# Cross attention of a decoder with its sums laid out by query tile: tokens on the partitions, no copy and turn of the sums, and their bias as a row added by GpSimd

## The reference

```
tn = _ln(t, norm_g, norm_b)
t = _mha(tn, tn, skv, sq, sow, sob, tgt_mask) + t     # self attention, 16 heads of 64
tn = _ln(t, norm_g, norm_b)
t = _mha(src, tn, ckv, cq, cow, cob, src_mask) + t    # cross attention, 77 keys
tn = _ln(t, pg, pb)
t = t + (jax.nn.relu(tn @ w1 + b1) @ w2 + b2)         # 128 -> 512 -> 128
```

## Time and profile before

| | |
|---|---|
| median of 3 runs | 1062.11 us (1061.4 to 1063.75) |
| the profiled execution, its own time | 1062.09 us |
| its span in the profile | 1060.0 us |
| TensorE busy | 1025.4 us (97%) |
| ScalarE busy | 811.6 us (77%) |
| VectorE busy | 717.0 us (68%) |
| GpSimd busy | 393.8 us (37%) |

### The profile page before, as it was taken

How to read it: one execution, slowest core, us unless ns; L and a number is a source line. 1 busy time by engine, 2 the same in 40 slices (tenths; PEclk the granted TensorE clock), 3 DMA queues, 4 the chain that set the end, 5 groups by cost and what they waited for, 6 DMA issues and landing times.

```text
span 1060.0 us, 20691 instructions
## 1 busy us (share of the span) xinstructions
PE 1025.4 (97%) x5236; PEld 615.5 (58%) x5236; DVE 717.0 (68%) x4485; ACT 811.6 (77%) x3540; POOL 393.8 (37%) x407
## 2 busy tenths in 40 slices
PE   8899999999999999999999999999999999999996
PEld 6655556565456665545655555656655566555565
DVE  4766786556788566778665578655678755677845
ACT  4787997576998576899666799766799867689852
POOL 4233443233443233443333344323344323344322
PEclk9999999999999999999999999999999999999999
DMA  8322000003000002200003200001300000000000
GB/s 235 88 61 68 1 21 2 1 20 109 20 21 1 2 1 80 68 2 21 1 2 80 68 1 21 1 1 33 103 14 21 2 1 1 21 1 1 2 1 24
DMA packets 31818, 32.39 MB, mean 31 GB/s; under 512 B 3998, under 2 KB 27726, under 8 KB 30926
## 3 DMA queue, kind: packets, MB, share of 16 engines
q1 hardware_dynamic: 29390, 28.80, 9.4%
q10 hardware_dynamic: 2304, 2.20, 0.7%
HBM read 30.47 MB, written 0.52 MB: 29 GB/s over the span
## 4 chain that ended last, share of the span: by engine, by line
PE 86%; DVE 8%; issue 3%; ACT 1%; DVEq 1%; POOL 1%; POOLq 0%
PE S L1090 23%; PE T L1102 12%; PE sum L1132 10%; PE W L901 8%; PE sum L1116 7%; PE W L956 4%; PE W L925 4%; PE W L843 3%; PE W L880 3%; PE W L863 2%; PE W L858 2%; PE W L920 2%; DVE XN L1468 2%; DVE Pb L1620 2%; PE W L834 2%
## 5 line engine op out<-in xcount | busy, mean ns | idle before, releaser
L1382 ACT ACTIVATE Pb<-Pb,mn 128x128 f32<-128x128 f32 (+1 forms) x1536 | 560.5, 370 | 42.4 <-DVE mn L1620 42.1
L708 POOL TENSOR_TENSOR Pb<-Pb,rsum 128x512 f32<-128x512 f32 (+2 forms) x336 | 325.4, 971 | 582.3 <-DVE rsum L1628 582.3
L1382 ACT ACTIVATION_READ_ACCUMULATOR Pb<-Pb,mn 128x1 f32 x1536 | 293.0, 191 | 0.0
L1620 DVE CUSTOM_DVE_ANT_0 Pb<-S,late_bias 128x128 f32<-128x128 f32 x768 | 175.6, 285 | 130.4 <-PE S L1090 130.1
L1102 PEld LDWEIGHTS T<-ident,Pb 128*128 128x128 f32 (+2 forms) x1296 | 163.9, 146 | 155.1 <-issue 119.7
L1090 PE MATMUL S<-GV,XT 128*128 128x512 f32 x384 | 199.6, 607 | 1.6 <-DVE mn L1620 0.8
L1102 PE MATMUL T<-ident,Pb 128*128 128x128 f32 (+2 forms) x1296 | 197.4, 273 | 1.2 <-POOL Pb L708 1.2
L1638 DVE COPY PT<-T 128x512 f32<-128x512 f32 (+1 forms) x240 | 156.3, 651 | 57.1 <-PE T L1102 55.7
L1620 DVE CUSTOM_DVE_ANT_0 Pb<-S,cross_bias 128x77 f32<-128x77 f32 x768 | 132.4, 232 | 70.4 <-PE S L1090 68.0
L1132 PE MATMUL sum<-PT,Vc 128*128 128x512 f32 (+2 forms) x264 | 134.4, 599 | 0.0
L1090 PE MATMUL S<-Gc,XT 128*128 128x462 f32 (+1 forms) x288 | 126.7, 521 | 0.6 <-DVE mn L1620 0.5
(11 more groups left out here) (213 smaller groups left out, 1071.1 us busy)
## 6 DMA issues: line engine op xcount, KB each, us to landing
sakv<-in_L_xattn_sa_kv SPq DMA_DIRECT2D x6, 1024.0 KB, 5.0
caq<-in_L_xattn_ca_q SPq DMA_DIRECT2D x6, 512.0 KB, 8.0
saq<-in_L_xattn_sa_q SPq DMA_DIRECT2D x6, 512.0 KB, 6.2
cakv<-in_L_xattn_ca_kv SPq DMA_DIRECT2D x12, 256.0 KB, 7.8
saow<-in_L_xattn_sa_ow SPq DMA_DIRECT2D x6, 512.0 KB, 4.0
w<-in_L_xattn_ff_w SPq DMA_DIRECT2D x12, 256.0 KB, 3.0
caow<-in_L_xattn_ca_ow SPq DMA_DIRECT2D x30, 96.0 KB, 2.5
GV<-in_mask_BxSxS_ik ACTq DMA_DIRECT2D x1, 1536.0 KB, 9.3
```

Source lines behind the costliest of these rows:

```text
L708: nc.gpsimd.tensor_tensor(rows, rows, r, ALU.mult).then_inc(sem(f"{unit.name}_weights"), 1)
L1382: last = nc.scalar.activation(Pb[:, s, t * w:(t + 1) * w], Pb[:, s, t * w:(t + 1) * w], ACT.Exp, bias=mn[:, s, t:t + 1], scale=-1.0, accum ...
L1620: last = nc.vector.tensor_tensor_reduce(out=Pb[:, s, cols], in0=S_ps[n % 2][:, cols], in1=row_bias, scale=1.0, scalar=3.4e38, op0=ALU.add, ...
```

## The change

Cross attention goes by query tile. `place_of` gives each chunk its group and tile: in the cross phases the three groups of one tile follow on each other, then the next tile's. `attend_tokens(n)` runs after each turned chunk: the turned weights of one tile are the stationary operand, the values `Vc` move (128 columns), and the sums have tokens on the partitions. For this, ScalarE's copy and the job `fin` of the cross phases are left out; VectorE adds `sum_ps` to `X` itself (`cross_residual`), and this add now frees the bank. The bias `ca_ob` is loaded as a row to all partitions (`cob`) and added to `X` by GpSimd after the norm in front of the cross attention. The counterpart is done in `ending`. Some places on the tick list are changed too. `vT` shares the memory of `o_pair` (used in the other path only).

```diff
-CV0_AT = (13, 15, 18, 20, 26, 30)
-CV_AT = (4, 6, 7, 22, 26, 29)
-SELF1_AT = (23, 25, 26, 30)
+CV0_AT = (10, 12, 15, 16, 24, 27)
+CV_AT = (4, 6, 7, 20, 26, 29)
+SELF1_AT = (23, 24, 26, 30)
-WEIGHTS0_AT = (5, 3, 7, 10, 13, 16)
-WEIGHTS_AT = (20, 25, 30, 32, 33, 33, 35, 35, 38, 38, 40, 40, 43, 42, 45, 45)
-AFTER_S0 = (3, 4, 5, 5, 8, 9)
+WEIGHTS0_AT = (5, 3, 7, 12, 16, 18)
+WEIGHTS_AT = (20, 23, 30, 32, 33, 33, 35, 35, 37, 37, 40, 40, 43, 42, 45, 45)
+AFTER_S0 = (3, 4, 5, 5, 6, 7)
-LAST_AT = (1, 3, 5, 7)
+LAST_AT = (1, 3, 5, 9)
-FEED1 = ((9, 9, 9, 9), 10, (18, 18, 20, 21))
+FEED1 = ((9, 9, 9, 9), 12, (18, 18, 20, 21))
...
+            if self.groups[first].cross:
+                qt, group = divmod(n - first * TB, len(XHEADS))
+            self.place_of.append((self.groups[first + group], qt))
...
-            for blk in range(group.blocks):
+            for blk in range(TB):
+                if group.cross:
+                    self.attend[max(self.tick_of[g * TB + blk] + 1 + spread[group.phase % 4], self.start[group.j, group.phase % 4] + 5)].append((g, blk))
+                    continue
...
-        self.jobs[at + steps[1]].append(("fin", j, b, cross))
+        if not cross:
+            self.jobs[at + steps[1]].append(("fin", j, b, cross))
...
-                        if event[0] == "xn" and event[3] == 2 and step == STEPS - 1:
+                        if event in unit.biased and step == STEPS - 1:
...
-                            nc.gpsimd.tensor_tensor(rows, rows, b2[:, j, :].unsqueeze(1).broadcast_to([P, TB, E]), ALU.add)\
-                              .then_inc(sem(f"{unit.name}_b2"), 1)
+                            held = (b2 if w == 2 else cob)[:, j, :]
+                            nc.gpsimd.tensor_tensor(rows, rows, held.unsqueeze(1).broadcast_to([P, TB, E]), ALU.add)\
+                              .then_inc(sem(f"{unit.name}_biased"), 1)
...
+                def attend_tokens(n):
+
+                    group, qt = unit.place_of[n]
+                    j, b, g = group.j, group.b, n // TB
+                    pe.wait_ge(sem(f"{unit.name}_turned_sb{n % 2}"), l * (C // 2) + n // 2 + 1)
+                    if group.first and qt == 0:
+                        pe.wait_ge(sem(f"{unit.name}_oT"), l * unit.phases + group.phase)
+                        made(ring, [("cV", j, b, i) for i in range(3)], l)
+                    for blk in range(group.blocks):
+                        k = group.starts[blk + 1] - group.starts[blk]
+                        mm = nc.tensor.matmul(sum_ps[:, qt * P:(qt + 1) * P], PT[0:k, g % 2, blk, n % TB * P:(n % TB + 1) * P],
+                                              Vc[0:k, b, group.block0 + blk, :], start=(group.first and blk == 0),
+                                              stop=(group.last and blk == group.blocks - 1))
+                    if n % TB == TB - 1:
                         mm.then_inc(sem(f"{unit.name}_attended"), 1)
...
-                for i in range(2):
-                    pe.wait_ge(sem("tail_oT"), i + 1)
-                    for t in range(TB // 2):
-                        c = (i * TB // 2 + t) * P
-                        last = nc.tensor.transpose(T_ps[i][:, t * P:(t + 1) * P], oT[:, 1, c:c + P], ident[:])
-                    last.then_inc(sem("tail_turned"), 1)
...
+                        if k // B == 1:
+                            continue
...
+                def cross_residual(phase):
+
+                    j, b = phase // 4, phase % B
+                    rows = X[:, batch(b), :]
+                    last_group = max(g for g, x in enumerate(unit.groups) if x.phase == phase)
+                    dve.wait_ge(sem(f"{unit.name}_attended"), l * len(unit.groups) + last_group + 1)
+                    dve.wait_ge(sem(f"{unit.name}_biased"), l * len(unit.biased) + unit.biased.index(("xn", j, b, 1)) + 1)
+                    nc.vector.tensor_tensor(rows, tiles(sum_ps[:]), rows, ALU.add).then_inc(sem(f"{unit.name}_oT"), 1)
```

More of the change, by code:

```diff
@@ L173, in __init__ @@
         self.phases = 4 * layers
+        self.place_of = []
+        for n in range(self.chunks):
+            first = next(g for g, x in enumerate(self.groups) if x.phase == self.groups[n // TB].phase)
+            group, qt = divmod(n - first * TB, TB)
+            if self.groups[first].cross:
+                qt, group = divmod(n - first * TB, len(XHEADS))
+            self.place_of.append((self.groups[first + group], qt))
         self.first_group = [next(g for g, x in enumerate(self.groups) if x.phase == k) for k in range(self.phases)]
@@ L199, in __init__ @@
         self.norms = [e for t in range(self.ticks) for e, step in self.norm[t] if step == STEPS - 1]
+        self.biased = [e for e in self.norms if e[0] == "xn" and e[3] > 0]
         self.score_at, self.exp_at, self.sum_at = ([[] for _ in range(self.ticks)] for _ in range(3))
@@ L202, in __init__ @@
         for n in range(self.chunks):
-            group = self.groups[n // TB]
+            group, qt = self.place_of[n]
             made = ("G", group.j, group.b, group.index)
@@ L1119, in attend @@
                         return
+                    if group.cross:
+                        attend_tokens(g * TB + blk)
+                        return
                     k = group.starts[blk + 1] - group.starts[blk]
@@ L1125, in attend @@
                             pe.wait_ge(sem(f"{unit.name}_oT"), l * unit.phases + group.phase)
[L1126 to L1130, removed]
+                        made(ring, [("V", j, b, group.index)], l)
                     at_end = blk == group.blocks - 1
-                    mm = nc.tensor.matmul(sum_ps[:], vals, PT[0:k, g % 2, blk, :],
+                    mm = nc.tensor.matmul(sum_ps[:], V[0:k, group.v_slot, blk, :], PT[0:k, g % 2, blk, :],
                                           start=(group.first and blk == 0), stop=(group.last and at_end))
                     if at_end:
+                        mm.then_inc(sem(f"{unit.name}_attended"), 1)
+                def attend_tokens(n):
+                    group, qt = unit.place_of[n]
+                    j, b, g = group.j, group.b, n // TB
[9 more added lines that the diff above has]
+                    if n % TB == TB - 1:
                         mm.then_inc(sem(f"{unit.name}_attended"), 1)
@@ L1264, in work @@
                             act.wait_ge(sem("small_in"), N_SMALL + 144 * l)
[L1265 removed]
+                        g, bb = small[:, j, 1:2], small[:, j, 2:3]
                     else:
@@ L1282, in work @@
                     _, _, b, f = event
-                    last = nc.scalar.activation(hT[:, f, :], w[:], ACT.Relu, bias=small[:, j, 4 + f:5 + f])
+                    last = nc.scalar.activation(hT[:, f, :], w[:], ACT.Relu, bias=small[:, j, 3 + f:4 + f])
                 last.then_inc(sem(ring.free(event)), 1)
@@ L1413, in decoder @@
                             act.wait_ge(sem("small_in"), N_SMALL + 144 * l)
-                        nc.scalar.activation(oT[:, k % B, :], sum_ps[:], ACT.Identity, bias=small[:, j, k // B:k // B + 1])\
+                        nc.scalar.activation(oT[:, k % B, :], sum_ps[:], ACT.Identity, bias=small[:, j, 0:1])\
                           .then_inc(sem(f"{unit.name}_oT"), 1)
@@ L1419, in ending @@
             def ending():
-                act.wait_ge(sem("fast_attended"), len(FAST.groups))
                 for i in range(2):
[L1423 to L1426, removed]
+                    act.wait_ge(sem("tail_turned"), 1 + i)
                     nc.scalar.activation(XT[:, T:2 * T][:, cols2(i)], S_ps[i][:, 0:T // 2], ACT.Identity,
-                                         bias=small[:, L - 1, 3:4], scale=small[:, L - 1, 2:3]).then_inc(sem("tail_xt"), 1)
+                                         bias=small[:, L - 1, 2:3], scale=small[:, L - 1, 1:2]).then_inc(sem("tail_xt"), 1)
                 for i in range(2):
@@ L1664, in decoder @@
                             scaled_values("L3", b)
+                    for phase in unit.evict_o[t]:
+                        if phase % 4 // B == 1:
+                            cross_residual(phase)
                     for event, step in unit.norm[t]:
@@ L1704, in added @@
                     return nc.vector.tensor_tensor(X[:, ts, :], tiles(bank[:, 0:n * P]), X[:, ts, :], ALU.add)
+                dve.wait_ge(sem("fast_attended"), len(FAST.groups))
+                dve.wait_ge(sem("fast_biased"), FAST.biased.index(("xn", L - 1, 1, 1)) + 1)
                 for i in range(2):
-                    dve.wait_ge(sem("tail_turned"), i + 1)
-                    added(tiles2(i), T_ps[i])
+                    nc.vector.tensor_tensor(X[:, tiles2(i), :], tiles(sum_ps[:, cols2(i)]), X[:, tiles2(i), :], ALU.add)
                     variances(tiles2(i), EPS_DEC)
```

57 lines of the change are left out of this document (28 added, 29 removed).

## The result

| | us |
|---|---|
| before, median of 4 runs beside it | 1061.76 (1061.04 to 1063.75) |
| changed, median of 4 runs | 1042.64 (1041.94 to 1044.44) |
| ratio | 0.9818, 95% interval 0.9803 to 0.9833 |
| span of the profiled execution, before and changed | 1060.0 and 1039.9 |

The change makes the kernel 1.8% faster: 19.1 us, where 5.9 were forecast and 11.6 (to 1050.5 us) was the most that the stated range allowed. The direction was right, the size was not.

The account below looks back on a forecast made before the run. The prediction took TensorE, busy for 97% of the span, as the bound in the layers and a latency chain at the end. Its terms summed to -5.9 us from 1062.09, giving 1056.2 us, range 1050.5 to 1063.5.

Parts of the forecast that it names:

- sums, 528 for 132 matmuls: Cross phases: 528 matmuls of 128 columns, priced like those of `out`, replace 132 of 512; +4.3 us.
- bare starts of the runs: First weight load of each of 144 chunks' runs may not be hidden; +2.0 us, bounds 0 and +17.
- fin gone, with its waits: Four transposes removed in 11 decoder places, -4.8 us; dearer cases -1.2; one wait for ScalarE's copy -0.4.
- wait at x0 + 6: TensorE's wait for VectorE's normalised rows before batch 1's cross-attention `xn`, six layers, covered by earlier sums; -3.5 us.
- wait at `cv`: Tick x1 + 7, five layers: bank freed earlier by a shorter chain, though the bank ring shifts; half of -4.5, -2.2 us.
- GpSimd's adds: Twelve bias adds of 1.27 us queued ahead of the next chunk's weights; +1.0 us, bounds 0 and +15.
- moved places: Moved weights and batch 1's `out` change the order of TensorE's pieces, not their number; 0, 2 us either way.
- the end: After the last turned chunk VectorE reads the sums directly, so the first add starts earlier; -1.1 us.
- the burst as a cover: First four chunks' sums on tick x0 + 5 delay TensorE some 2.5 us, so the rows for `xn` are ready; -3.5 us.
- The rivals with bare starts: Slower: every chunk's run of sums starts with its weight load unhidden; 17 us in place of 2, 1071 us; 8%.
- with the load as the bound: Slower: all 1056 records of the sums run at the weight load's 190 ns; +83 us, 1139 us; 3%.
- with GpSimd in the way: Slower: bias adds hold up the weights at ticks s1 + 7 and x0 + 6; up to 15.3 us, 1070.5 us; 9%.

Follow-up runs that it names:

- run 6: Changed kernel with the sums of x0's first four chunks spread over ticks x0 + 5, 6, 7 and 7, not all on x0 + 5: 1046.31 us, ratio 0.9846.
- run 9: Changed kernel with the first sums of x1 held back to tick x1 + 9, as before the change: 1047.91 us, ratio 0.986.
- run 8: Changed kernel with GpSimd's cross-attention bias add cut to one column of 128, all waits kept: 1041.32 us, ratio 0.9798.
- run 1: Changed kernel with all eight rows of places on the tick list as before the change: 1047.66 us, ratio 0.9856.
- run 2: Kernel before the change with only the eight new rows of places: 1056.94 us, ratio 0.9952.
- run 11: Changed kernel with the jobs' rows CV_AT, SELF1_AT and WEIGHTS_AT as before the change: 1047.23 us, ratio 0.9845.
- run 4: Changed kernel with four unused identity transposes per cross phase at fin's places, and a one-column ScalarE copy emptying their bank: 1045.64 us, ratio 0.9843.
- run 5: Changed kernel with ScalarE's copy, four unused turns at fin's place and VectorE's add of the copy behind the decoder's cross sums: 1054.73 us, ratio 0.9923.
- run 12: Changed kernel without the filling matmuls (FILL 0 in place of 3) in front of batch 0's feed-forward xn: 1033.97 us, ratio 0.9725.

## Why the prediction was wrong

By its own steps, in us:

| step | forecast | measured | from |
|---|---|---|---|
| sums, 528 for 132 matmuls | +4.3 | +6.1 in all | start to start, 115.2 and 121.3, each pair with a wait counted without it |
| bare starts of the runs | +2.0 | in the line above; 0.5 of it | three chunks of 144 |
| fin gone, with its waits | -6.4 | -6.5 | start to start: 5.1 of records, 1.4 in front |
| wait at x0 + 6 | -3.5 | -4.5 | start to start; run 6 gives 3.7 back |
| wait at `cv` | -2.2 | -4.8 | start to start; run 9 gives 5.3 back |
| GpSimd's adds | +1.0 | +1.3, unsure, inside the other lines | run 8 |
| moved places | 0, 2 either way | -5.0 | runs 1 and 2 |
| the end | -1.1 | -1.13 | chain |
| in front of `xn` behind the fill | none | -1.4 | start to start |
| in front of cross scores, behind turns and behind scores | none | -2.6 | start to start |
| the wait at the head of the next layer's s0 | none | +1.0 | start to start |

Without GpSimd's line these are -18.8 us, for 19.1 measured (20.1 between the two profiled executions).

**Right.** TensorE was the bound, its clock never fell, the price of 128 columns was that of `out` (the chain's runs of sums are at 0.89 and 0.67, as forecast), fin, the end, the burst as a cover, and the small price of GpSimd's adds. The sums cost 6.1 us for 6.3 forecast, though not quite as forecast: a block of one group costs eight records of 0.1117 us where it cost two of 0.4314, about 4.1 us in all; three chunks start late (0.5); the rest stands where `cv` and `xn` now follow the sums. The rivals with bare starts (17 us), with the load as the bound (83) and with GpSimd in the way are out. The rule of the Trainium skill on small matmuls (page "TensorE: Matmul & The Clock Gate", section "Back-to-back issue gap") would make the new sums 2.5 times the old; the trace differs: 121.3 against 115.2 us, a ratio of 1.05, and the measurement decides.

**Wrong: the moved places, the largest miss.** The prediction said they "change the order of PE's pieces, not their number; 0, with 2 us either way". The same argument had just been used for the burst, where moving work of unchanged length in front of a wait was counted as a gain. The wait in front of the next layer's `xn` in s0 stood in the row of waits for normalised rows, 6.7 us of which the text took 3.5 and never asked for the other half. Runs 1, 2 and 11 show it: 5.0, 5.4 and 4.6 us, with that wait five times in the traces of runs 1 and 11, never in the change's and once in run 2's, with 0.17 us. Two microseconds of bound for a part that reaches 3 us of listed waits was too small.

**Wrong: the wait at `cv`, in size and in cause.** I named the shorter chain behind the sums and the ring, and took half. Runs 4 and 5 put back each of these and the wait stayed away; run 9, which only moves sums, brings all of it back. It is the same mechanism as at x0 + 6: the sums by tile let TensorE begin a phase's sums after its second chunk in place of its fourth, so 2.5 us of work stand in front of the wait. The prediction had the tick list from which this follows and looked at x0 alone.

**Wrong: waits priced at the idle time shown.** Start to start a wait of 0.61 cost 0.78 and one of 0.89 cost 0.96. With no wait a record starts while the one before it still runs, 0.43 us and 0.20 us after its start at these two places; behind the wait it starts after the whole record and the wait, 1.20 and 1.16 us. Short extra times went too that were in no term: in front of `xn` behind the fill (1.4), and in front of cross scores (2.6: 1.5 behind turns, and 1.1 behind other scores, where no idle time shows and the cause is open). Together some 5 us. Against them stands the wait at the head of the next layer's s0, which grew from 0.16 (once 0.11) to 0.35 us in five layers; in layer 3's chain 0.86 us of sums stand in front of it where 1.05 stood, so the two together are 1.21 us as before.

**Where the layout's 14.7 us come from** is shown in its parts (turns, both covers, the end), but what the runs that undo one part cost does not add to the gain: the direct add 12.1 (run 5), the two covers 3.7 and 5.3, the places 5.0, 26 us in all for 19.1. For run 5 the reason is ScalarE's full queue in x0; for the others it was not taken apart. Open: what the direct add is worth with fin at a later tick, and which of the three job rows does the places' work.

## What to carry to other kernels

Where one engine is busy for 97% and its idle time is many short waits, the order of its work is worth as much as its amount: list every repeated wait, and for each ask what independent work the change puts in front of it, the moved jobs included. Splitting an accumulation so that its first parts can run early gives such work, at a price that here was 5% of the sums' own time, 6.1 us. After such a change look again at everything that was put in to bridge a gap: the fill of 8.0 us had become plain work, and taking it out paid nearly half as much as the change.

## What the runs showed of the hardware that I had not expected

Four matmuls of 128 columns with a new stationary operand each cost 1.05 times one of 512 over 528 of them (121.3 and 115.2 us start to start, waits left out), and 1.04 within a run (0.1117 and 0.4314 us a record). In either form the second record behind a job of matmuls with 64 rows starts 0.10 us late, 15 times in each trace, so that loss did not grow with four times as many loads. And without the fill in the layers, with waits of up to 0.5 us, the granted clock stayed at 1.00 from 45 to 1000 us (run 12).
